# One burst of 32-row matmuls for all score maxima of a half image, in four lent PSUM banks, with new orders on all engines

## The reference

```
win    = 8x8 windows of x as (B*16, 64 tokens, 128)
normed = layernorm(win) ; q, k, v = split(normed @ in_w.T + in_b)
scores = q k^T / sqrt(16) per head (8 heads of 16) ; attn = softmax(scores)
y      = win + (attn v) @ out_w.T + out_b
y      = y + silu(layernorm(y) @ fc1_w.T + fc1_b) @ fc2_w.T + fc2_b       (hidden 256)
# second layer, linear attention over N = 1024 tokens of an image, E = 64
out    = wo @ ((q2 k2 / N) v2) + bo + y
```

## Time and profile before

| | |
|---|---|
| median of 3 runs | 365.84 us |
| profiled execution | 366.59 us |
| its span | 364.8 us |
| TensorE matmul busy | 348.3 us (95%), 3424 instructions |
| TensorE weight loads busy | 299.3 us (82%) |
| VectorE busy | 285.1 us (78%) |
| ScalarE busy | 245.6 us (67%) |
| GpSimd busy | 166.9 us (46%) |
| mean granted TensorE clock | 0.988 |

### The profile page before, as it was taken

The page is one execution under the profiler, slowest core; times in us unless marked ns, Lnnn a source line. Parts: engine busy times, 40 slices in busy tenths (PEclk is TensorE's granted clock), DMA queues, the critical chain, the costliest instruction groups (busy, mean ns, idle before and its releaser), DMA issues. The chain is left out here.

```text
span 364.8 us, 9920 instructions
## 1 busy us (share of the span) xinstructions
PE 348.3 (95%) x3424; PEld 299.3 (82%) x3424; DVE 285.1 (78%) x850; ACT 245.6 (67%) x449; POOL 166.9 (46%) x177
## 2 busy tenths in 40 slices
PE   7899899999999999999999999999999999999875
PEld 6788788888888888888888888878888888878563
DVE  5676888888788878798788888888788878867652
ACT  5557776775959477674968658684877659684360
POOL 6513575444455434635445433646444443622430
PEclk9999999999999999999999999999999999999995
DMA  4242130303222131302123031212123031210011
GB/s 133 67 100 63 33 97 4 91 29 82 76 60 72 29 86 58 86 29 72 63 67 86 14 101 58 70 45 58 58 72 101 0 86 58 60 31 2 0 60 58
DMA packets 31859, 21.99 MB, mean 60 GB/s; under 512 B 22432, under 2 KB 23776, under 8 KB 31840
## 3 DMA queue, kind: packets, MB, share of 16 engines
q1 hardware_dynamic: 31744, 21.62, 21.7%
q10 hardware_dynamic: 96, 0.13, 0.1%
HBM read 4.95 MB, written 4.19 MB: 25 GB/s over the span
## 5 line engine op out<-in xcount | busy, mean ns | idle before, releaser
L526 POOL TENSOR_TENSOR hid_l<-hid,hid_h 128x512 fp32r<-128x512 f32 x30 | 40.4, 1369 | 37.1 <-ACT hid_h L1136 35.3
L706 PE MATMUL p_score<-kd_h,qd_h 128*128 128x128 f32 (+1 forms) x512 | 55.8, 252 | 1.6 <-DMA qd_h<-q_h 1.5
L706 PEld LDWEIGHTS p_score<-kd_h,qd_h 128*128 128x128 f32 (+1 forms) x512 | 49.9, 163 | 6.9 <-DVE row_max L1344 1.7
L1102 ACT ACTIVATE probs<-p_scoreT 128x512 f32<-128x512 f32 x64 | 38.6, 603 | 24.5 <-PE p_scoreT L729 24.4
L1344 DVE TENSOR_REDUCE row_max<-p_score 128x8 f32<-128x512 f32 x64 | 44.0, 687 | 14.1 <-PE p_score L706 14.0
L744 PEld LDWEIGHTS p_attn<-vd,probs 128*64 128x64 f32 x1024 | 36.2, 139 | 16.2 <-issue 9.0
L744 PE MATMUL p_attn<-vd,probs 128*64 128x34 f32 x1024 | 45.4, 244 | 1.7 <-ACT probs L1102 1.7
L531 POOL TENSOR_TENSOR y_l<-y,y_h 128x512 fp32r<-128x512 f32 x15 | 19.3, 1285 | 60.2 <-ACT y_h L1116 60.2
L518 POOL TENSOR_SCALAR kd_l<-k_l,head_a 128x512 fp32r<-128x512 f32 x15 | 23.6, 1572 | 35.7 <-DVE k_l L1326 21.3
L725 PE MATMUL p_scoreT<-qd_h,kd_h 128*128 128x256 f32 x128 | 39.5, 309 | 0.0
L510 POOL TENSOR_TENSOR rstd<-rstd,minus_half 128x4 f32<-128x4 f32 (+1 forms) x33 | 35.5, 1075 | 2.7
(11 more groups left out here) (262 smaller groups left out, 915.5 us busy)
## 6 DMA issues: line engine op xcount, KB each, us to landing
qd_l<-q_l SPq DMA_DIRECT2D x64, 64.0 KB, 2.0
vd<-v_tok SPq DMA_DIRECT2D x64, 64.0 KB, 2.2
qd_h<-q_h SPq DMA_DIRECT2D x62, 64.0 KB, 2.0
out<-out_sb SPq DMA_DIRECT2D x15, 256.0 KB, 2.0
x_in<-in_x SPq DMA_DIRECT2D x14, 256.0 KB, 2.7
x_first<-in_x SPq DMA_DIRECT2D x2, 256.0 KB, 2.8
fc_rows<-in_L_conv_fc_w SPq DMA_DIRECT2D x2, 128.0 KB, 2.6
out<-out_sb SPq DMA_DIRECT2D x2, 128.0 KB, 2.1
```

The lines of the kernel that those rows point to most:

```text
L526: pool.tensor_tensor(hid_l[:, t], hid[:, t], hid_h[:, t].bitcast(F32), ALU.subtract).then_inc(hid_low[t], 1)
L706: last = pe.matmul(p_score[0:rows, 2 * KEYS * j:2 * KEYS * (j + 1)], qd_h[:, h.par, j, 2 * KEYS * p:2 * KEYS * p + rows], kd_h[:, h.par, 2 ...
L1102: act.activation(probs[:, p % 2], p_scoreT[:].rearrange("row (win j q) -> row win j q", win=2, j=QUADS), ACT.Exp, scale=SCORE_SCALE).then_ ...
```

## The change

The scores for the maxima of all four pairs of a half are made in one burst of 32 matmuls at the start of the half. Each uses the 32 rows of one head pair j, of `q_h` and of `kd_h`, and not the spread copy. The head pairs write to four banks; pair p has 128 columns of each. The four banks are those of stages a and d: `p_x[:, 0..3]` are now `p_a[0]`, `p_a[1]`, a new `p_n` (transpose of x, layer norm of stage a) and `p_d`. `p_score` is gone, and its uses in the prologue and the epilogue move to `p_scoreT` and `p_n`.

```
-        row_max = sb("row_max", [128, 2, HEADS])
-        max_wide = sb("max_wide", [128, 2, HEADS, KEYS], BF16)
+        row_max = sb("row_max", [128, PAIRS, HEADS])
+        max_wide = sb("max_wide", [128, PAIRS, HEADS, KEYS], BF16)
...
-        p_score = bank("p_score")
+        p_x = ctx.enter_context(nc.psum_tensor("p_x", [128, QUADS, 512], F32))
+        p_a, p_n, p_d = [p_x[:, 0], p_x[:, 1]], p_x[:, 2], p_x[:, 3]
...
+        def norm_banks(h): return p_c if h.second() else [p_n, p_a[1]]
+        def q_bank(h):     return p_c[0] if h.second() else p_a[0]
+        def k_bank(h):     return p_c[1] if h.second() else p_a[1]
+        def score(p):      return p_x[:, :, 2 * KEYS * p:2 * KEYS * (p + 1)]
...
+            def b_score(h, with_a):
+                pe.wait_ge(q_high, h.n())
+                pe.wait_ge(kd_high[0], h.n())
+                pe.wait_ge(kd_high[1], h.n())
+                pe.wait_ge(v_kept, h.n())
+                pe.wait_ge(k_low, h.n())
+                if not h.follows(1):
+                    pe.wait_ge(bias_kept, 1)
+                elif with_a:
+                    pe.wait_ge(xn_tok_set, h.n(-1))
+                if h.second():
+                    pe.wait_ge(ob_kept, 1)
+                for win, columns in ((1, 2 * KEYS), (0, KEYS)):
+                    for p in range(PAIRS):
+                        for j in range(QUADS):
+                            rows = slice(32 * j, 32 * j + 32)
+                            last = pe.matmul(score(p)[0:columns, j], q_h[rows, 2 * KEYS * p:2 * KEYS * p + columns],
+                                             kd_h[rows, h.par, 2 * p + win], start=True, stop=True)
+                last.then_inc(score_ready, 1)
+
+            def scores_read(h):
+                for p in range(PAIRS):
+                    pe.wait_ge(max_ready[p], h.n())
```

More of the change, by code:

```diff
@@ L307, in norm_banks, with q_bank, k_bank, score @@
         def norm_banks(h):
-            return p_c if h.second() else p_a
+            return p_c if h.second() else [p_n, p_a[1]]
+        def q_bank(h):
+            return p_c[0] if h.second() else p_a[0]
+        def k_bank(h):
+            return p_c[1] if h.second() else p_a[1]
+        def score(p):
+            return p_x[:, :, 2 * KEYS * p:2 * KEYS * (p + 1)]
         def images(eng, prologue, step_even, step_odd, epilogue):
@@ L624, in load_qkv_weights @@
                 for k in range(3):
[L625 removed]
+                    last = pe.transpose(p_scoreT[:, C * k:C * k + C], in_w_rows[:, k, :], ident[:])
                 last.then_inc(wT_ready, 1)
@@ L690, in a_v, with b_scoreT @@
                 last.then_inc(v_ready, 1)
-            def b_score(h, p):
+            def b_score(h, with_a):
+                pe.wait_ge(q_high, h.n())
+                pe.wait_ge(kd_high[0], h.n())
[18 more added lines that the diff above has]
+                    pe.wait_ge(max_ready[p], h.n())
+            def b_scoreT(h, p):
                 if p == 0:
                     pe.wait_ge(q_high_dma, h.n(times=16 * QUADS))
[L697 to L713, removed]
                     pe.wait_ge(q_low_dma, h.n(times=16 * QUADS))
@@ L901, in step @@
                 if with_a and with_c:
+                    a_k(a)
+                b_scoreT(b, 1)
+                if with_a and with_c:
                     a_q(a)
[L903 to L906, removed]
                 if with_d:
                     d_kvT(loop, -1)
-                b_attn(b, 1)
+                b_attn(b, 0)
+                b_scoreT(b, 2)
+                if with_d:
+                    d_bT(loop, -1)
+                if with_c:
+                    c_back(c)
+                b_attn(b, 1)
+                if not with_c:
+                    load_weights()
+                b_scoreT(b, 3)
+                if with_d:
+                    d_mT(loop, -1)
+                b_attn(b, 2)
                 if with_a:
@@ L934, in step @@
                     load_biases()
+                if with_d:
+                    pe.wait_ge(fin_kept[1], loop.image(-1))
             def step_even(loop, more, c):
@@ L1045, in first_xn, with a_xn_high, a_xn_full @@
                 last.then_inc(xn_full, 1)
-            def a_xn(h):
+            def a_xn_high(h):
                 act.wait_ge(xnT_ready, h.n())
[L1049 to L1056, removed]
+                act.wait_ge(q_ready, h.n(1))
+                act.wait_ge(k_ready, h.n(1))
+                for v in range(2):
+                    last = act.activation(in_windows(xn_h[:], v), in_rows(p_a[1][:], v), ACT.Copy)
+                last.then_inc(xn_high, 1)
+            def a_xn_full(h):
+                act.wait_ge(v_ready, h.n(1))
+                for v in range(2):
+                    last = act.activation(in_windows(xn[:], v), in_rows(p_a[1][:], v), ACT.Copy)
+                last.then_inc(xn_full, 1)
             def a_q(h):
@@ L1471, in step @@
                 b_max(b, 0)
+                b_max(b, 1)
+                if with_c:
+                    c_o(c)
+                b_max(b, 3)
+                if not with_c:
+                    a_k(a)
+                b_max(b, 2)
                 b_widen(b, 0)
```

237 lines of the change are left out of this document (108 added, 129 removed).

## The result

The changed kernel took 375.67 us (median of 4 runs, 374.18 to 378.14) against 366.31 us for the kernel before in the same sessions: ratio 1.026, 95% interval 1.023 to 1.029. It is slower by 9.4 us. Forecast were 358 us and, with a chance of 0.73, a faster kernel; the range ended at 370.

A forecast was written before the change was run, and what follows sets the result against it. TensorE's own order was taken as the bound. Steady part -10.7, start +1.4, end +2.1 against the profiled 366.59 us gave 359.4, or 358.6 at the median; less for mode switches, 358 us, range 349 to 370.

The forecast's parts named there:

- What bounds the kernel, and the burst: Steady part: TensorE's own order is the bound; the 32-matmul burst takes 1.1 us, saving 1.9 us a half.
- Rival B: Burst: the 32-row loads go in turn, so it takes 3.0 us and the whole 379 us; chance 0.10.
- mode switches: Switches around the old score bursts, which go too; for them the forecast was lowered from 358.6 to 358 us.
- It waits 1.4 us: TensorE ahead of fc2, behind an even half: waits 1.4 us for hidden's low part from GpSimd.
- 0.7: TensorE ahead of fc2, behind an odd half: waits 0.7 us for hidden's low part from GpSimd.
- The clock ... so I charge nothing.: TensorE's clock: waits of 0.7 to 1.4 us leave it as busy as a full-clock half, so no cost.
- DMA ... costs nothing while that 0.75 holds.: SP's queue: the next x load lands at t+8.9, its transpose wants it at t+9.65, so no cost.
- start term: Halves 0 and 1: half 2 starts at about 53.4 us instead of 52.01, +1.4 us.
- The start's other terms: Half 0's burst starts at 17.6 us, its last maximum comes at 22.6, the second burst at 35.9.
- A sign of being wrong: The forecast is wrong if the transpose of x or the maxima show TensorE's largest wait.
- End ... +2.1: Last half: from burst to last scoreT 14.6 us against 12.5, +2.1, with waits for fc2, y1 and yn.
- D: Steady halves: one more link late by 0.6 us in each of 13 halves, 366 us, no change; chance 0.20.

The follow-up runs named there:

- rows128: Changed kernel's order and banks, but the burst made of the old 128-row matmuls from the spread copy of q: 394.73 us, ratio 1.076 to the kernel before.
- twice: Changed kernel with the burst of 32-row matmuls made twice over: 375.61 us, ratio 1.027 to the kernel before.
- x_early: Changed kernel with the x load of half 3 issued by SP in the prologue: 368.65 us, ratio 1.005 to the kernel before.
- best_a: Changed kernel with early x load, last half's old order, filler matmuls ahead of fc2 and in halves 0 and 1: 361.87 us, ratio 0.987 to the kernel before.
- fill: Changed kernel with 24 unused bf16 matmuls ahead of fc2 in odd halves and the last one: 371.49 us, ratio 1.013 to the kernel before.
- best_b: As best_a, with v of half 1 also ahead of the weights in half 0: 360.41 us, ratio 0.9815 to the kernel before.
- fills_only: Changed kernel with all of best_b's filler matmuls and none of its orders: 370.78 us, ratio 1.011 to the kernel before.
- kv_late: Changed kernel with VectorE's normalisation of y put back ahead of kv in the last half: 373.15 us, ratio 1.020 to the kernel before.

## Why the prediction was wrong

Point by point, in its own steps.

- **What bounds the kernel, and the burst.** Right. Measured 0.83 us for the 1.1 taken, between the bounds of 0.63 and 3.0. rows128 shows that the gain is overlap: single loads and matmuls kept their lengths. Rival B, that the loads go in turn, is out: 32 loads of 181 ns fit into 0.83 us. That it is the four different row parts which let them overlap is the likely reading; no run puts the same 32-row matmuls into one row part in turn. The "mode switches" for which the sum was lowered by 0.6 have no row of their own: in twice the second burst costs 0.70 and the first with it 0.83, which leaves 0.13 for going in and out.
- **"It waits 1.4 us" and "0.7"** ahead of fc2: measured 1.56 and 0.25. GpSimd's hid_l releases both, and "the wait takes up what the burst costs" holds as long as there is wait (twice). The even half came out at 17.92 for 17.95 by errors that cancel: the burst and the wait for fc2 are 0.7 less than taken, the wait for the maxima (0.34) and the other blocks (16.49 for 16.15) 0.7 more. The odd half was 22.8 for 22.17, most of it the 0.5 to 0.6 ahead of the next burst. Over the stretch from half 2's burst to the last one that is 3.1 us (262.2 in x_early, which has no dips, against 259.1). This step was right in kind and small by 3 us.
- **"The clock ... so I charge nothing."** This step failed. I compared busy shares of whole halves and found a half with 1.0 us idle of 18.05 at full clock. The half compared with has its idle time in pieces of 0.75 us at most. The changed kernel has it in pieces of 1.5 to 2.5 us, and in or right behind such a piece TensorE fell from 2.4 to 1.2 GHz, in some halves and not in others. In the profiled execution half 2, half 3 and half 11 lost 1.2 to 1.6 us each in this way, 4.0 together (266.2 against x_early's 262.2). Half 1 lost up to 2.8 (20.31 us in x_early at 0.77, against my 17.5 for the same waits); that this is all clock is an estimate, for which speaks that best_a's half 1, at 0.85, took 1.3 less. The last part lost some 3. fill, twice, best_a, best_b and fills_only show it for the odd halves and the last one: with matmuls in the gap, or a shorter gap, no fall is left there.
- **"DMA ... costs nothing while that 0.75 holds."** I walked SP's queue for steady halves only, where it held. In half 1 the load stands behind a copy of v that the change makes late (35.61 on ScalarE, forecast 35.3) and behind five loads of biases (38.91 to 41.7) that the prediction doesn't mention. Cost: 2.9 us (x_early). My start term was +1.4 for half 2's burst; it was at 59.75 and not at 53.4: 2.9 the load, 0.6 the later second burst, and up to 2.8 the clock in half 1.
- **The start's other terms** held: first burst 17.90 (17.6), wait for the maxima in half 0 2.31 us, second burst 36.51 (35.9). A sign of being wrong that the prediction names, the transpose of x or the maxima among the largest waits, did show in halves 0 and 1 (2.31 and 2.48 us, beside 2.50 ahead of the second burst).
- **"End ... +2.1".** The wait for yn was 1.92 (2.1 forecast), for y1 0.88 (0.9), for fc2 1.57 (1.4), in the right places. The end was +5.3 all the same. The surplus of 3.2 is nearly all clock, which fell behind the waits for fc2 and for yn: kv_late gives back 1.1 beyond the wait itself, fill 1.7. With both, best_b's last part is 43.22.
- **The rivals.** What happened is nearest to D, more links late, but its price was not a late link in each half: it was two events at the start and the clock, which fell behind some of the long waits. None of the four had the clock in it, though the sum itself named idle pieces of 1.4, 1.5 and 2.1 us. The failed row was a mean over a half, where what mattered was how the idle time lies together.

Put together on the span: forecast 359.4 - 1.8 = 357.6, measured 374.2. The miss of 16.6 is 6.3 before half 2's burst (59.75 against 53.4), 7.1 from there to the last one (266.16 against 259.1: 4.0 of it the three dips, 3.1 the waits), and 3.2 behind it (48.29 against 45.1). Of the 16.6, some 10 are the clock, 2.9 the x load, and 3.7 waits that were taken too short.

## What to carry to other kernels

A faster block on the busiest engine turns work into idle pieces, and on TensorE they can have a second price, the clock behind them: here pieces of 1.5 us or more, and two of 0.7 to 0.8 close together. Look for where idle time lies together in the new order, not for the mean, and fill it with matmuls that compute nothing if it can't be removed. When a block is moved forward, walk each queue that feeds it in the first and the last passes as well as in the steady loop; one-time loads stand in front there. When an edit that must help makes things slower, look at the clock of the stretch before judging it: v ahead of the weights seemed to cost 4.5 us on top of x_early and gave 1.5 with the fillers in place (best_b against best_a), and all cures together gave 15.

## What was not expected of the hardware

- Behind idle pieces of 1.5 us the clock fell in some halves and not in others of the same length, in one execution (halves 3 and 11 of the changed kernel, not 5, 7, 9 or 13, all waiting 1.56 to 1.57 us). What picks them is open. That makes runs of one kernel spread: 365.5 to 370.9 us in nine runs of x_early, against 361.0 to 362.4 in six of best_a, whose gaps are filled in odd halves and in half 0.
- The clock also fell where no single piece was long: in best_b at 34.4 us behind waits of 0.72 and 0.77, and in the kernel before at 356.2 us behind waits of 0.52, 0.52 and 0.42, all within a few us. In the kernel before single waits of 0.69 and 0.75 (at 32.4 and 40.2 us) left it at 1.00.
- Thirty-two matmuls of 32 rows with 32 different loads, into four banks, took 0.83 us, 26 ns each, below the 40 ns of the attention block's in the earlier trace rows, though each load by itself took 181 ns.
- VectorE's maximum over 512 elements took 680 ns when it read them from four banks in one instruction, and 687 from one.
